# Four more tiles of x normalised on ScalarE, and the opening's orders written anew

## The reference, cut to what matters

```python
xn = _layernorm(x, axis=-1)            # (x - m) / sqrt(v + eps)
s  = _L0_attn_ref(xn, wq, wk, wv, wo)  # 32 query heads, 8 key/value heads of 128
g  = _silu(_L0_ffn_ref(xn, router_w, A, B))
x  = x + s * g
```

## Time and profile before

| | us |
|---|---|
| median of three runs | 1318.01 |
| lowest and highest | 1316.51, 1318.69 |
| the profiled execution | 1316.54 |
| its span in the profile | 1314.7 |
| PE busy in the span | 1292.5 |
| DVE, ACT, POOL busy | 966.9, 956.1, 455.0 |

### The profile page before, as it was taken

One profiled execution on the slowest core, in us unless ns is written; L12 is line 12 of the kernel. 1 busy time (PEld: TensorE's weight loads), 2 busy tenths in 40 slices (PEclk: granted clock), 3 DMA queues, 4 the chain that ended last, 5 costly groups with the idle time before them and its releaser, 6 DMA issues.

```text
span 1314.7 us, 22709 instructions
## 1 busy us (share of the span) xinstructions
PE 1292.5 (98%) x6920; PEld 1096.2 (83%) x6920; DVE 966.9 (74%) x2444; ACT 956.1 (73%) x2500; POOL 455.0 (35%) x365
## 2 busy tenths in 40 slices
PE   7899999999999999999999999999999999999998
PEld 6688788888888888888888888888888888888886
DVE  6976678777777677777777777777777767777776
ACT  5777577877777776778677777777677867776874
POOL 5413311413215242333424235151432534234323
PEclk9999999999999999999999999999999999999999
DMA  6000000101101011010000101010110101012124
GB/s 224 25 9 21 23 11 9 65 24 49 41 25 41 6 36 23 16 32 24 24 19 21 24 24 38 10 36 5 31 32 8 40 8 35 21 40 89 49 84 149
DMA packets 69617, 48.99 MB, mean 37 GB/s; under 512 B 48577, under 2 KB 48833, under 8 KB 69569
## 3 DMA queue, kind: packets, MB, share of 16 engines
q1 hardware_dynamic: 66976, 44.00, 12.0%
q10 hardware_dynamic: 2592, 4.40, 0.9%
HBM read 34.74 MB, written 8.39 MB: 33 GB/s over the span
## 4 chain that ended last, share of the span: by engine, by line
PE 91%; DVE 4%; ACT 2%; issue 1%; DMA 1%; POOL 1%; SPq 0%; DVEq 0%; ACTq 0%
PE bank_b L570 19%; PE bank_a L570 18%; PE bank_b L667 13%; PE o_ps L667 13%; PE pv_ps L660 10%; PE pair L644 7%; PE pair L651 6%; PE pair L640 2%; PE pair L642 1%; PE o_ps L570 1%; DMA x_sb<-x 1%; DVE pT_lo L1420 0%; DVE stats L1252 0%; PE bank_a L630 0%; DVE cosx L1388 0%
## 5 line engine op out<-in xcount | busy, mean ns | idle before, releaser
L445 POOL TENSOR_TENSOR rot<-rot,tab 128x512 f32<-128x512 f32 x160 | 207.1, 1296 | 522.8 <-ACT rot L978 522.5
L1027 ACT ACTIVATE probs<-probs,row_min 128x128 f32<-128x128 f32 (+1 forms) x512 | 225.6, 446 | 1.0 <-DVE row_min L1431 0.8
L1046 ACT ACTIVATE pT_hi<-pair 128x768 fp32r<-128x768 f32 x128 | 103.6, 810 | 159.3 <-PE pair L651 158.6
L1038 ACT ACTIVATE probs<-probs,row_inv 128x128 f32<-128x128 f32 (+1 forms) x512 | 190.6, 445 | 11.3 <-DVE row_inv L1450 10.5
L1420 DVE TENSOR_TENSOR pT_lo<-pair,pT_hi 128x768 fp32r<-128x768 f32 x128 | 122.1, 954 | 87.5 <-ACT pT_hi L1046 86.8
L570 PE MATMUL bank_a<-xT_hi,w_hi 128*128 (+1 forms) x376 | 150.0, 399 | 0.1
L428 POOL TENSOR_TENSOR w_hi<-raw,zero 128x512 fp32r<-128x512 f32 x74 | 84.5, 1142 | 188.8 <-PE bank_a L570 107.4
L570 PE MATMUL bank_b<-xT_hi,w_hi 128*128 (+1 forms) x376 | 149.8, 398 | 0.0
L570 PE MATMUL bank_a<-xT_hi,w_lo 128*128 (+1 forms) x376 | 146.8, 391 | 0.0
L570 PE MATMUL bank_b<-xT_hi,w_lo 128*128 (+1 forms) x376 | 146.8, 390 | 0.0
L570 PE MATMUL bank_a<-xT_lo,w_hi 128*128 (+1 forms) x376 | 146.3, 389 | 0.0
(11 more groups left out here) (185 smaller groups left out, 3287.0 us busy)
## 6 DMA issues: line engine op xcount, KB each, us to landing
raw<-w_seq SPq DMA_DIRECT2D x76, 256.0 KB, 2.7
b_raw<-v_T SPq DMA_DIRECT2D x320, 16.0 KB, 1.8
gate_scratch<-b_raw ACTq DMA_DIRECT2D x16, 256.0 KB, 2.0
out<-y_sum SPq DMA_DIRECT2D x16, 256.0 KB, 2.0
x_sb<-x SPq DMA_DIRECT2D x3, 1024.0 KB, 11.0
mid<-x SPq DMA_DIRECT2D x7, 256.0 KB, 2.6
mid<-gate_scratch SPq DMA_DIRECT2D x7, 256.0 KB, 2.8
raw<-x SPq DMA_DIRECT2D x7, 256.0 KB, 2.7
```

Source lines behind the costliest of these rows:

```text
L445: nc.gpsimd.tensor_tensor(v, v, tab[:, s:s + SEQ].unsqueeze(1).to_broadcast([P, 2, SEQ]), ALU.mult).then_inc(sin_done[kind], 1)
L1027: a = nc.scalar.activation(s, s, ACT.Exp, bias=row_min[:, j % 2, i:i + 1], scale=-1.0, accum_out=row_sum[:, i:i + 1])
L1038: a = nc.scalar.activation(s, s, ACT.Copy, scale=row_inv[:, i:i + 1])
L1046: nc.scalar.activation(pT_hi[:, :, :], pair[j % 2][:, :, 0:ROWS], ACT.Copy).then_inc(pThi_done, 1)
```

## The change

Tiles 8 to 11 move from `ON_DVE` to `ON_ACT`. DVE's `normalise(8, 12, 6)` goes (four L1270); `shifts(8, 12, 5)` on DVE and `x_shifted(8, 12, 5)` on ACT (four L1130) come, the latter behind `x_high(7)` and ahead of `copy_vT(1)`. The three hand-written lists are written in a new order; apart from that, the same calls stand in them. PE's and SP's lists are the same, instruction for instruction.

```diff
-ON_ACT = (0, 1, 2, 4, 5, 6, 7)
-ON_DVE = (3,) + tuple(range(8, TILES))
+ON_ACT = (0, 1, 2) + tuple(range(4, 12))
+ON_DVE = (3,) + tuple(range(12, TILES))
...
             def pool_opening():
                 sin_product(K, 1)
                 first_low(WQ + 1)
+                first_low(WQ + 2)
+                first_low(WV)
                 inverse_std(1)
-                first_low(WQ + 2)
                 sin_product(H0, 1)
                 inverse_std(2)
-                first_low(WV)
                 first_low(WQ + 3)
+                split(0, WO)
+                split(0, WO + 1)
                 sin_product(H1, 1)
                 sin_product(H2, 1)
+                inverse_std(3)
                 sin_product(H3, 1)
...
@@ act_opening
             x_high(6, first_banks[6])
             x_high(7, first_banks[7])
-            k_high(1, None)
+            x_shifted(8, 12, 5)
+            copy_vT(1, None, FIRST_V)
             q_high(H1, 1, None)
-            copy_vT(1, None, FIRST_V)
             swap_halves(H3, FIRST_H3, 1, H1, 1)
...
@@ dve_opening
-            cos_product(K, bank_a, 1)
             shifts(4, 8, 4)
             cos_product(H0, bank_b, 1)
+            cos_product(K, bank_a, 1)
+            rotate(H0, 1)
             rotate(K, 1)
-            rotate(H0, 1)
+            block_statistics(3)
             x_low(4, first_banks[4])
             x_low(5, first_banks[5])
             q_low(H0, 1)
+            shifts(8, 12, 5)
...
-            normalise(8, 12, 6)
```

More of the change, by code:

```diff
@@ L1153, in act_opening @@
             first_high(WQ + 2)
-            swap_halves(H0, bank_b, 1, None, None)
             first_high(WV)
             first_high(WQ + 3)
+            swap_halves(H0, bank_b, 1, None, None)
             x_shifted(4, 8, 4)
             swap_halves(H1, pv_ps, 1, H0, 1)
+            swap_halves(H2, o_ps, 1, K, 1)
             x_high(4, first_banks[4])
@@ L1172, in act_opening @@
             v_high(1, None, pv_ps)
-            swap_halves(H0, bank_b, 2, H3, 1)
+            q_high(H2, 1, None)
             exponents(0, 1)
@@ L1212, in act_opening @@
             low_scores(1, 6)
+            attn_high(3, 4, None)
             normalise_rows(0, 5)
-            attn_high(3, 4, None)
             exponents(1, 6)
@@ L1618, in dve_opening @@
             cos_product(H3, bank_b, 2, H1, 2)
+            rotate(H2, 2)
             q_low(H2, 2)
-            row_inverse(4)
             rotate(H3, 2)
             dve_side(0, 2, 1)
+            cos_product(K, bank_a, 3, H2, 2)
+            q_low(H3, 2)
             mask_rows(0, 5)
+            rows_low(3, 4)
             attn_low(2, 3)
-            q_low(H3, 2)
-            rows_low(3, 4)
-            cos_product(K, bank_a, 3, H2, 2)
             cos_product(H0, bank_b, 3, H3, 2)
+            mask_rows(1, 6)
+            row_inverse(5)
+            rotate(H0, 3)
             add_tile(0, 1, start=True, bank=o_ps[:, :])
-            row_inverse(5)
-            mask_rows(1, 6)
-            rotate(K, 3)
             attn_low(3, 4)
             add_tile(1, 2, start=True, bank=bank_b[:, :])
-            rotate(H0, 3)
             row_inverse(6)
+            rotate(K, 3)
             v_low(2)
```

88 lines of the change are left out of this document (42 added, 46 removed).

## The result

The changed kernel took 1320.68 us (median; 1320.01 to 1321.53), the kernel before in the same comparison 1317.04 us: the ratio is 1.0028, with a 95% interval of 1.0019 to 1.0037. That is 3.6 us slower. The prediction had 4.75 us slower, and its 1322.8 us is 2.1 us above what was measured; 1.0 us of that is that the three runs it set out from lay above the later median. 1320.68 us is also what rival 1 had (1320.7), and it lies 0.3 us under the range that the prediction gave its likeliest case (1321.0 to 1324.5); as a difference, 3.6 us stands midway between the forecast's 4.75 and rival 1's 2.65.

The account below looks back on a forecast made before the run. PE, busy 1292.5 of 1314.7 us, was taken as the bound, so only its waits count. Terms 3.3 + 1.65 - 0.2 = +4.75 us on the median 1318.01 gave 1322.8 us, range 1317.3 to 1325.2.

Parts of the forecast that it names:

- rival 1: Front: POOL's power blocks like any product, small shift and masked row never ask; +2.65 us, 1320.7; chance 0.15.
- likeliest case: The forecast itself, blocked shifts and rotations in the opening: +4.75 us, 1322.8, own range 1321.0 to 1324.5; chance 0.50.
- Steps 1 and 2: Front: held shift of tiles 4 to 7 and two held rotations make tile 6's turn 2.7 us late.
- the rule on two SBUF inputs: DVE instructions with two SBUF inputs contend with GpSimd instructions reading SBUF; the loser waits for the whole instruction.
- Step 3: Tiles 8 to 11: held shift, then ACT's four tiles stand bare; first scores at 40.6, 3.65 us late.
- Step 4, the first term: Up to `turn_probs(0)`: some lateness is given back, so it comes at 50.35 for 47.08, +3.3 us.
- Step 5, the second term: Unit 0's new order: V's projection 14.25 behind `turn_probs(0)`, side tile 11 19.55 behind; +1.65 us.
- Step 6, the third term: Behind side tile 11: the 0.17 wait goes, -0.2 us; no new PE wait over 0.4 between 75 and 95.
- Rivals 1 and 2: Front: small shifts never ask; power blocks in 1 (+2.65 us, 0.15), lets go in 2 (+1.5 us, 1319.5, 0.20).
- Rival 3: Unit 0: H1's later cosine product does no harm, V's projection within 13.0 of `turn_probs(0)`; 1315.6 us; chance 0.10.
- Rival 4: Unit 0's waits also set back unit 1's rows: 2 to 3 us more, 1325.5; chance 0.05.

Follow-up runs that it names:

- filled kernel: Changed kernel with small identity matmuls on PE in four waits of the opening (12, 2, 2 and 5): 1320.35 us, 1.0029 against the kernel before.
- filled one that overran: Changed kernel with 24 small identity matmuls on PE ahead of the turn of tile 6: 1322.62 us, 1.0034 against the kernel before.
- fronts-only one: Changed kernel with POOL's list and the later parts of ACT's and DVE's as before, tiles 8 to 11 on ACT: 1318.66 us, 1.0011 against before.
- kernel before with new second parts: Kernel before with only the later part of the three lists in the new order, tiles 8 to 11 on DVE: 1322.2 us, 1.0043 against before.

## Why the prediction came out right, point by point

**Steps 1 and 2, the front: shown.** The shift of tiles 4 to 7 ended at 24.52 (predicted 24.3) and took 1.24; both rotations were over 1 us; `x_low(4)` at 32.15 (32.45); wait ahead of tile 6 3.35 (about 3.7), turn at 32.88 (33.15). Two causes that the prediction named are borne out by taking each away: the statistics put late again gave 1.5 us at tile 6, and POOL's old list between 1.2 (race lost) and 3.9 us (race won). The second rotation of the kernel before was held as well, so the rotations were no new cost; what was new was the late inverse and the held shift. And L1260, which the prediction counts as bearing out the rule on two SBUF inputs, reads one SBUF tensor: it was held 1.27 us, but it isn't a case of that rule.

**Step 3: right in its times.** Second shift 1.23 us, ACT's four tiles from 35.38 (35.7), first scores at 40.18 (40.6). The prediction said that the moved work stands bare there. With the tiles left on DVE the scores came at least 0.65 earlier, starts counted, and with half of the tiles behind the swap of H3 0.8 earlier than with all four ahead of it, so a part of their 2.94 us is bare. How much of the 3.2 us of lateness is that work and how much the order isn't separated: with all four on ACT and POOL's old list the scores came 1.7 earlier than before where the race was won, and 1.75 later where it was lost.

**Step 4, the first term: mis-sized.** +3.3 predicted, +2.80 measured, or about 2.5 without the start's 0.27. `x_low(4)`, the first scores and `turn_probs(0)` came 0.30, 0.42 and 0.47 before their forecasts, or 0.57, 0.69 and 0.74 with the start's 0.27: the waits were the right ones, and most of the error is there at `x_low(4)`. The second rotation ended at 28.71 (28.8), and the `w_lo` that holds the add of eps at 32.21 (32.4); with the start taken off, each is some 0.4 ahead of its forecast.

**Step 5, the second term: right in size, not in independence.** V's projection 14.45 behind `turn_probs(0)` (14.25), side tile 11 19.40 behind (19.55), so +1.5 for +1.65. But the kernel with this part alone lost 5.9 us: 3.0 us because DVE's four L1270 stood in POOL's splits, and 1.9 by `turn_probs(0)`, behind a low clock that the prediction had no term for. Four fewer L1270 were "worth nothing more" in the prediction; that holds against the old POOL list only.

**Step 6, the third term: mis-sized.** -0.2 predicted. The wait at the earlier trace rows's last row did go, with lateness falling from 4.32 to 3.49, so -0.8: the 0.17 of that row, and short gaps of up to 0.3 us in the kernel before that no row marks. By 94.54, with a new wait of 0.33, lateness was back at 3.92. So the small sum of this step came out near by luck: two errors of about half a microsecond each that cancel. I had said that no such wait over 0.4 would come, and none did.

The clock was missed: at 3.35 us of waiting ahead of tile 6 it fell to 0.50, and the sum had no term for it. It cost nothing here that the totals can tell, which the filled kernel shows; in the filled one that overran, in the fronts-only one, and in the kernel before with new second parts it stood bare. The Trainium skill, TensorE: Matmul & The Clock Gate, section "HAM oscillation — how this bites in real kernels", says that a PE that idles long enough drops to the slow clock and starts its next stretch of matmuls cold. The trace agrees: 1.97 us for a turn of 1.25, then 0.78 and 0.63 for matmuls of 0.48 and 0.40. It was a reason to set a rival with the clock beside the sum.

Rivals 1 and 2 needed a small shift that never asks for the port: two shifts of 1.24 and 1.23 us beside sine products rule them out. That rival 1's total is the measured one is chance: its first shift was to run at 23.1 and tile 6 to be 1.45 late, and it was 2.42. Its other half, that the power blocks, is ruled out by the rotations that ran inside it. Rival 3 needed V's projection within 13.0 of `turn_probs(0)`: 14.45. Rival 4's delay of unit 1's rows was 0.33 us.

What stays open: why the clock falls behind 1.20 us of waiting in one kernel and not behind the same waits of the kernel before, and whether the race at 18 us is what parts the two groups of runs of the fronts-only kernel.

## What to carry to other kernels

Before moving an instruction with two SBUF inputs on DVE or any on POOL, look at what the other engine has in progress at the moment it asks, and not only at durations: two orders of POOL made the same four instructions 1.91 and 5.53 us. Look also for places where the two ask within a few tenths of each other: there one launch can differ from the next, and a profile shows only one of them. When a wait is shortened, follow the gain to the next wait on the same path before counting it; twice here it was spent there (the late statistics, and the filled changed kernel). And parts of a hand-written order that depend on each other can't be undone one by one: half the change lost more than the whole.
